# A softmax inside one attention stage: scores evacuated by ScalarE before the maximum, and a deeper software pipeline over the heads

## The reference, cut to what matters

```python
def _msa(x, w_qkv, w_proj):
    b, n, d = x.shape
    qkv = (x @ w_qkv).reshape(b, n, 3, H, DK)        # H = 16 heads, DK = 64
    ...
    attn = jnp.einsum('bhnd,bhmd->bhnm', q, k) * (1.0 / np.sqrt(DK))
    attn = jax.nn.softmax(attn, axis=-1)             # over 2048 keys
    y = jnp.einsum('bhnm,bhmd->bhnd', attn, v)
    y = y.transpose(0, 2, 1, 3).reshape(b, n, d)
    return y @ w_proj
```

## Time and profile before

| | us |
|---|---|
| median of 3 runs | 46944.63 |
| lowest and highest of them | 46517.64, 47062.42 |
| profiled execution, its own time | 46143.25 |
| span of its slowest core | 46141.6 |
| spans of the eight cores | 45576.0 to 46141.6 |

### The profile page before, as it was taken

How to read it: one execution, slowest core, us unless ns; L and a number is a source line. 1 busy time by engine, 2 the same in 40 slices (tenths; PEclk the granted TensorE clock), 3 DMA queues, 4 the chain that set the end, 5 groups by cost and what they waited for, 6 DMA issues and landing times. The chain is left out here.

```text
span 46141.6 us, 395095 instructions; the slowest of 8 cores (45576.0 to 46141.6 us)
## 1 busy us (share of the span) xinstructions
PE 25886.9 (56%) x109783; PEld 10813.5 (23%) x109783; DVE 12688.2 (27%) x24675; ACT 6856.4 (15%) x15436; POOL 7273.3 (16%) x8069
## 2 busy tenths in 40 slices
PE   2265014555888788895334433333333277777778
PEld 0022001211333233331211122212221033333333
DVE  2221431113444344442442233333332100000001
ACT  0022100100111011110111222222221011111111
POOL 1134851311111111111001000000000111111111
PEclk6687557777998789886556555555555688888888
DMA  0122121222111122111000000000001222222221
GB/s 32 45 75 73 62 71 56 89 64 72 61 61 55 47 67 63 55 52 49 7 11 32 22 2 2 2 12 2 2 2 38 78 66 66 66 66 66 66 66 64
DMA packets 1063111, 2173.71 MB, mean 47 GB/s; under 512 B 151297, under 2 KB 408332, under 8 KB 1056844
## 3 DMA queue, kind: packets, MB, share of 16 engines
q1 hardware_dynamic: 847500, 1499.59, 10.6%
q0 software_dynamic: 213504, 648.84, 3.9%
HBM read 1591.49 MB, written 556.34 MB: 47 GB/s over the span
## 5 line engine op out<-in xcount | busy, mean ns | idle before, releaser
L979 PE MATMUL pb<-e_h,e_wd 128*128 128x512 bf16 x16384 | 4342.0, 415 | 1099.2 <-DVE e_h L61 960.3
L61 ACT ACTIVATE e_h<-pb 128x512 bf16<-128x512 f32 x4096 | 2446.3, 597 | 16074.8 <-PE pb L961 8371.3
L1683 PE MATMUL pb<-e_xg,e_wu 128*128 128x512 bf16 x16384 | 3563.5, 380 | 1941.9 <-POOL e_wd L61 1817.1
L1405 PE MATMUL pb<-sb_idb,ma_pr 128*128 128x128 bf16 x8192 | 1740.9, 270 | 4702.2 <-ACT ma_prT L61 2669.4
L961 PE MATMUL pb<-e_xf,e_wu 128*128 128x512 bf16 x16384 | 3947.6, 403 | 0.1
L1707 PE MATMUL pb<-e_h,e_wd 128*128 128x512 bf16 x16384 | 3546.4, 379 | 48.6 <-ACT e_h L61 33.2
L61 DVE TENSOR_TENSOR e_acc<-e_acc,pb 128x512 f32<-128x512 f32 x4096 | 2818.7, 688 | 2241.1 <-PE pb L979 2226.0
L499 PE MATMUL pb<-pj_xk,pj_w 128*128 128x512 bf16 x8192 | 1839.8, 389 | 1252.9 <-POOL pj_xk L61 1252.9
L1683 PEld LDWEIGHTS pb<-e_xg,e_wu 128*128 128x128 bf16 x16384 | 1606.7, 98 | 3889.7 <-issue 1968.5
L979 PEld LDWEIGHTS pb<-e_h,e_wd 128*128 128x128 bf16 x16384 | 1462.2, 102 | 3978.8 <-issue 3338.1
L61 DVE TENSOR_TENSOR e_h<-e_h,pb 128x512 bf16<-128x512 bf16 x2048 | 1408.8, 688 | 3201.6 <-ACT e_h L61 3201.5
(11 more groups left out here) (299 smaller groups left out, 24619.2 us busy)
## 6 DMA issues: line engine op xcount, KB each, us to landing
e_wsg<-L_ffn_W_up SPq DMA_DIRECT2D x1024, 256.0 KB, 2.8
e_wsg<-L_ffn_W_down SPq DMA_DIRECT2D x512, 512.0 KB, 4.0
e_wsg<-L_ffn_w POOLq DMA_DIRECT2D x512, 256.0 KB, 3.1
wstage<-L_ffn_w SPq DMA_DIRECT2D x512, 256.0 KB, 3.5
e_po<-s_pre_out SPq DMA_DIRECT2D x512, 256.0 KB, 2.8
s_pre_out<-e_po POOLq DMA_DIRECT2D x512, 256.0 KB, 2.4
e_xg<-s_xg SPq DMA_DIRECT2D x512, 128.0 KB
pj_win<-s_xn SPq DMA_DIRECT2D x256, 128.2 KB
```

Source lines behind the costliest of these rows:

```text
L61: inst = getattr(eng, opname)(*a, **kw)
L979: inst = nc.tensor.matmul(p.psum[b][:], wdn[par][fc][:, dc * 128:(dc + 1) * 128], hsb[fc][:], start=(fc == 0), stop=(fc == 3))
L1405: mmv = p.inc(nc.tensor.transpose(p.psum[b2][:].bitcast(BF16)[:, 0:128], probs[par][:, wc * 128:(wc + 1) * 128], cst["idb"][:]), "mm", 1)
L1683: inst = nc.tensor.matmul(p.psum[b][:], wu1[dc][:, fc * 128:(fc + 1) * 128], xgt[par][dc][:], start=(dc == 0), stop=(dc == DC - 1))
```

## The change

Scores no longer stay in PSUM until their exponentials are taken. A new function `emitEv` has ScalarE copy the four banks as f32 to an SBUF tile `sc_sb` (`ma_sc`, 2048 columns, four copies of it) and releases each bank as soon as it is copied. `emitMax` takes the place of `emitR`: one `reduce_max` over 2048 columns in SBUF. `emitX` becomes one `Exp` over 2048 columns, SBUF to SBUF, with one row sum, so `emitT2` has no sum to take. The loop is skewed: in step `h` the maximum is that of head `h - 1`, the exponentials and their scaling are those of head `h - 2`, and transposes and values are those of head `h - 3`, where it was `h`, `h` and `h - 2`.

```diff
+    sc_sb = [p.sbl(f"ma_sc{i}", [128, T], F32) for i in range(NP)]
-    nm4 = [p.sbl(f"ma_nm4{i}", [128, 4], F32) for i in range(NP)]
-    ss4 = [p.sbl(f"ma_ss4{i}", [128, 4], F32) for i in range(NP)]
+    ssum = [p.sbl(f"ma_ss{i}", [128, 1], F32) for i in range(NP)]
...
-            def emitR(h):
+            def emitEv(h):
                 par = h % NP
+                nc.scalar.wait_ge(p.sem("dv"), st["rm"][par])
                 for fq in range(4):
-                    nc.vector.wait_ge(p.sem("mm"), st["scmm"][h][fq])
-                    p.v("reduce_max", out=nm4[par][:, fq:fq + 1],
-                        in_=p.psum[fq][:], axis=AX.X, negate=True)
-                p.v("tensor_reduce", out=nmax[par][:], in_=nm4[par][:],
-                    axis=AX.X, op=ALU.min)
+                    nc.scalar.wait_ge(p.sem("mm"), st["scmm"][h][fq])
+                    p.s("activation", out=sc_sb[par][:, fq * TT:(fq + 1) * TT],
+                        in_=p.psum[fq][:], func=AF.Copy)
+                    p.bank_release(fq, "ac")
+                st["ev"][par] = p.cnt["ac"]
+
+            def emitMax(h):
+                par = h % NP
+                nc.vector.wait_ge(p.sem("ac"), st["ev"][par])
+                p.v("reduce_max", out=nmax[par][:], in_=sc_sb[par][:],
+                    axis=AX.X, negate=True)
                 p.v("tensor_scalar", out=nmax[par][:], in0=nmax[par][:],
                     scalar1=0.125, scalar2=None, op0=ALU.mult)
                 st["rm"][par] = p.cnt["dv"]
@@ emitX
-                for fq in range(4):
-                    p.s("activation", out=probs[par][:, fq * TT:(fq + 1) * TT],
-                        in_=p.psum[fq][:], func=AF.Exp, scale=0.125,
-                        bias=nmax[par][:], accum_out=ss4[par][:, fq:fq + 1])
-                    p.bank_release(fq, "ac")
+                p.s("activation", out=probs[par][:], in_=sc_sb[par][:],
+                    func=AF.Exp, scale=0.125, bias=nmax[par][:],
+                    accum_out=ssum[par][:])
@@ emitT2
-                p.v("tensor_reduce", out=rc[par][:], in_=ss4[par][:],
-                    axis=AX.X, op=ALU.add)
-                p.v("reciprocal", out=rc[par][:], in_=rc[par][:])
+                p.v("reciprocal", out=rc[par][:], in_=ssum[par][:])
@@
             for h in range(16):
                 emitA(h)
-                emitR(h)
-                emitX(h)
+                emitEv(h)
+                if h >= 1:
+                    emitMax(h - 1)
                 if h >= 2:
-                    emitB(h - 2)
-                emitT2(h)
+                    emitX(h - 2)
+                if h >= 3:
+                    emitB(h - 3)
+                if h >= 2:
+                    emitT2(h - 2)
+            emitMax(15)
+            emitX(14)
+            emitB(13)
+            emitT2(14)
+            emitX(15)
             emitB(14)
+            emitT2(15)
             emitB(15)
```

More of the change, by code:

```diff
@@ L1336, in phase_msaatt @@
     st = {"exp": [0] * NP, "rm": [0] * NP, "tc_mm": [0] * NP,
-          "scale": [0] * NP, "scmm": [[0] * 4 for _ in range(16)]}
+          "scale": [0] * NP, "scmm": [[0] * 4 for _ in range(16)],
+          "ev": [0] * NP}
     for s in range(NS):
```

## The result

The changed kernel takes 44498 us (median of 9 runs, 43875 to 45162) against 46852 us for the kernel before (10 runs): a ratio of 0.949, with a 95% interval of 0.9425 to 0.9554. The prediction was 44955 us. A second set of runs of the same two kernels on one chip gave 44465 against 46477 us, a ratio of 0.960 (0.956 to 0.963). The median of the changed kernel came out nearly the same both times, that of the kernel before 375 us lower. Some executions run slower on one half of the chip, the profiled one of the changed kernel among them, and only the ratios leave them out: the changed kernel's other runs lie at 44307 to 44498 us in the first set and at 43916 to 44091 in the second, so both kernels moved.

A forecast was written before the change was run, and what follows sets the result against it. A chain of waits round the engines was taken to bound the attention phase; ScalarE's waits, evacuations, exponential and copies sum to a 14.0 us step, 226.9 us a tile, 1990 us saved: 46944.6 - 1990 = 44955 us, range 43850 to 45800.

The forecast's parts named there:

- The likeliest case: Attention phase: ScalarE's queue sets a 14.0 us head step, 1990 us saved, 44955 us for the whole; chance 0.78.
- The wait for scores, 2.8 us from the last copy: Start of ScalarE's head step: evacuation waits for the new scores and starts about 2.8 us after its last copy.
- Four evacuations, 2.75 us: ScalarE's added PSUM-to-SBUF score copies: 4 x 0.69 = 2.75 us a head, ending at 5.5 us.
- The exponential at 2.00 + 0.18: ScalarE's single 2048-column exponential in place of four: 2.2 us, ending at 7.7; saves 1.3 us.
- Copies, 6.3: ScalarE's eight odd transpose copies at the end of a head step: 6.3 us, ending the step at 14.0.
- VectorE under cover by 1.3 us: VectorE reaches its first even copy at 6.4 us, ScalarE its first odd one at 7.7; VectorE's edits cost or save nothing.
- The tile, 226.9 us, and 1990 us in all: Query tile: 22.5 + 168 + 36.4 = 226.9 us for 289.1; 62.2 saved per tile, 1990 us in 32.
- both upper bounds: ScalarE's evacuations at 0.87 each add 360 us, its exponential at 3.48 adds 665 us.
- The clock rises: Rival: TensorE's clock leaves 0.50 in the attention phase, 1.4 us a step, 730 us less, so 44230; chance 0.08.
- The copy trains fall out of step: Rival: VectorE's even and ScalarE's odd copy intervals all become 1.12 us, 1150 us more, 46105; chance 0.06.
- The f32 tile stretches its users: Rival, slower side: sharing `ma_sc` stretches ScalarE's evacuations and exponential 2.4 times, step 20.2 us, 48150; chance 0.04.
- No wait ties the evacuation to the newest maximum: Rival denied here: some wait still ties ScalarE's evacuation to VectorE's newest maximum, step as before; given no chance of its own.

The follow-up runs named there:

- the run with a quarter more: Changed kernel with one more reduce_max per head, over 512 columns of the same tile; attention phase 7409 to 7414 us, 76 more than the changed kernel.
- the kernel with batched copies: Changed kernel with eight transposes gathered in each of banks 4 and 5 and one 1024-column copy from each, for sixteen of 128; phase 4755 to 4762 us.
- the kernel before with batched copies: Kernel before, with only the transposes gathered eight to a bank and two copies of 1024 columns; no evacuation or skew; phase 6602 to 6616 us.
- the reordered kernel: Changed kernel with gathered transposes, next scores ahead of value matmuls on TensorE, `ma_mo` copy behind the maximum; phase 3429 to 3441 us, ratios 0.888 and 0.884.

## Why the prediction was right

The likeliest case came about with its mechanism. By its steps:

1. *The wait for scores, 2.8 us from the last copy.* 2.83 us idle in most steps, 2.85 and 2.99 in the one shown. VectorE's start after a matmul in the earlier trace rows was a fair stand-in for ScalarE's.
2. *Four evacuations, 2.75 us.* 2.76: 597 ns each, as the sigmoid of the same shape had the earlier trace rows.
3. *The exponential at 2.00 + 0.18.* 2002 ns and 2.19 from its start to the first copy's, read off another stage's activation of the same width.
4. *Copies, 6.3.* 6.14 here, more where an interval is 1.12.
5. *VectorE under cover by 1.3 us.* The maximum took 2286 ns for the 2.29 extrapolated from the earlier trace rows, the cover was 1.30, and the run with the doubled maximum shows that it is real and where it ends.
6. *The tile, 226.9 us, and 1990 us in all.* 227.4 in the mean and 1970. That the two stores shown are 226.89 us apart, the sum to 0.01, is luck: tiles differ by 2 us, and in the step a wait 0.1 to 0.2 us longer stands against copies 0.16 shorter.

Three numbers in the prediction were off; none of them carries the forecast. The matmuls without a break in each step last 3.7 us (27014.64 to 27018.34), where it has 3.8. The forecast with both upper bounds is 44955 + 360 + 665 = 45980, where it ends the range at 45800. And the VectorE operation of 5635 ns was one of 64; others of them took 2350 with GpSimd at work beside them, the one at 4441.69 us for example.

The rule of the Trainium skill that was weighed against the change ("VectorE: DVE Perf Modes", table of perf modes) held for rates: the maximum got no cheaper per element in SBUF (685 ns for 512 columns in the run with a quarter more, 692 from PSUM before). What followed from it here, that the evacuation is pure loss, did not hold for the time, because the evacuation was work on an engine that had been idling 7.91 us a step. The run without skew gives the figure: in the old order a step went from 17.82 to 17.03 us. Counted from the end of ScalarE's last copy, the maximum starts at 5.7 us, 1.6 later than before, so only 1.6 of the evacuation's 2.8 us cost anything; the shorter maximum gives back 1.1 and the single exponential 1.3.

The rivals. *The clock rises*: it did not, 0.50 throughout, although TensorE's busy share went from 39% to 50%. *The copy trains fall out of step*: no; the first even copies ran ahead and after two intervals the trains were locked at 0.84. *The f32 tile stretches its users*: the exponential lay at 2001 to 2003 ns over 512 of them, the maximum at 2285 to 2287. *No wait ties the evacuation to the newest maximum*: 21 us of such waits in all.

What was off is the centre of the whole time: 44955 us stated, 44498 measured. The phase's own gain is off by only 20 us (34 in the mean of the cores), so the term that was mis-sized is the carry-over to the median. I subtracted from the median of three runs, 46945 us; ten runs placed it at 46852 and eleven others at 46477. In the second set 46477 less 1970 is 44507, for 44465 measured. In the first 46852 less 1970 is 44882, so some 380 us of the difference stay without an account, as said above.

## What to carry to other kernels

Where no engine is busy half the time, walk one step of the loop from the end of an engine's last instruction to the same point a step later, and add up: the sum, with durations from other stages' rows of the same shape, gave the phase's gain within 2%. A skew that lets each engine work on something finished a step earlier turns a chain into a queue, and added work is then free, up to its cover, on an engine that waits, and dear on the one that sets the pace; an extra operation per step on an engine tells which it is. Before skewing, look for small ping-pong copies: gathering eight transposes into a bank gained 2580 to 2680 us, more than the change studied, with or without it.

## What was not expected of the hardware

**TensorE's clock.** In the kernel with batched copies TensorE runs 5.6 us of matmuls without a break (29012.75 to 29018.34) in each step of 8.8 us (values, scores, then sixteen transposes), and its clock stays at 0.50. Reordered, at 6.06 us a step, it is 0.66 on average, alternating between the two levels (the window view of the two kernels, the first on core 3, the second on core 5, columns as in the first view above):

```profile
28000.00:30500.00 2500.00, 1506.19 (x9588) 990.89 (x9588) 1156.94 (x1600) 1475.38 (x1876) 72.08 (x136) 0.50 0.02 8
```

```profile
28500.00:29400.00 900.00, 637.85 (x4906) 439.77 (x4907) 592.19 (x819) 750.99 (x956) 33.91 (x64) 0.66 0.01 3
```

At the upper level sixteen value matmuls take 1.05 us for 1.88 at the lower (27019.39 and 27025.45 in the fence before), so my first rival, with 0.9 less, priced that part nearly rightly. In the kernel before with batched copies, with 5.5 us of matmuls without a break in a step of 12.4, the clock is 0.52 on average from 27000 to 32000 us, 0.50 in full steps and higher at the ends of tiles (sixteen value matmuls from 28895.12 take 1.21 us). "TensorE: Matmul & The Clock Gate" of the Trainium skill (Part 1) has activity release the throttle; here unbroken matmuls did not by themselves, and no run separates why.

**A core that gains in one expert stage can lose in the other.** In the profiled execution of the reordered kernel's first run, core 6 took 9193 us for the first layer's expert matmuls and 10005 for the second's, and core 4 10355 and 8925:

```profile
L961 PE MATMUL pb<-e_xf,e_wu x16384: 379/435/634, 11241.2 to 21596.5; 128*128 128x512 bf16 x200
L1707 PE MATMUL pb<-e_xg,e_wu x16384: 376/379/634, 31466.5 to 40391.5; 128*128 128x512 bf16 x200
```

(core 4; the medians of 435 and 379 ns go with the long and the short stage). The pattern recurs in pairs of cores in most runs here. The order of arrival alone does not explain it: in the profiled execution of the changed kernel run again, core 2 began its first-layer matmuls at 11071 us and took 9405, core 0 of the same die began at 11381 and took 9241. The cause stays open. It is why a phase's own length tells a change of this size better than the whole does.
